# Two grouped convolution stages on 16 image pairs: float32 expansions on 17-row blocks, and one tap of nine multiplied on GpSimd

## The reference

```python
r  = relu(((x @ Wr + br) - mean) * rsqrt(var + eps) * gamma + beta)   # 64 -> 16 channels per pixel
w  = (r @ Ws + bs).reshape(B, H, W, 16, 1, 9)                          # nine weights per pixel and group of 4 channels
xi = x @ Wi + bi                                                       # 64 -> 64 channels
patches = nine shifts of zero-padded xi, reshaped (.., 16, 4, 9)       # channel-major: index = shift * 64 + channel
out = sum(w * patches, axis=-1)
```

## Time and profile before

| | us |
|---|---|
| median of 3 runs (lowest to highest) | 686.87 (686.27 to 687.97) |
| the profiled execution, its own time | 687.15 |
| its span in the trace | 685.4 |
| first expansion of the last stage | 463.50 |
| PE busy over the span | 649.0 (95%) |
| DVE busy | 551.1 (80%) |
| ACT busy | 287.1 (42%) |
| POOL busy | 172.6 (25%) |

### The profile page before, as it was taken

How to read it: one execution, slowest core, us unless ns; L and a number is a source line. 1 busy time by engine, 2 the same in 40 slices (tenths; PEclk the granted TensorE clock), 3 DMA queues, 4 the chain that set the end, 5 groups by cost and what they waited for, 6 DMA issues and landing times.

```text
span 685.4 us, 14823 instructions
## 1 busy us (share of the span) xinstructions
PE 649.0 (95%) x6176; PEld 265.6 (39%) x6176; DVE 551.1 (80%) x901; ACT 287.1 (42%) x370; POOL 172.6 (25%) x156
## 2 busy tenths in 40 slices
PE   6867999999999999999999989999999999999995
PEld 7533333333333333333333333333444444444542
DVE  5699866989988988995577787848888888888885
ACT  3754622323231422143102400043677777677661
POOL 2100420009102700450041110411344234234230
PEclk9999999999999999999999999999999999999998
DMA  9920000000000000000000000000011121121122
GB/s 327 214 56 1 2 1 1 1 1 2 2 1 1 2 1 1 1 2 1 1 13 4 1 1 2 1 1 1 20 44 33 42 52 33 34 60 33 32 62 63
DMA packets 54511, 19.67 MB, mean 29 GB/s; under 512 B 51154, under 2 KB 51892, under 8 KB 54452
## 3 DMA queue, kind: packets, MB, share of 16 engines
q1 hardware_dynamic: 54164, 18.57, 11.2%
q10 hardware_dynamic: 288, 0.21, 0.1%
HBM read 10.39 MB, written 8.39 MB: 27 GB/s over the span
## 4 chain that ended last, share of the span: by engine, by line
PE 72%; DVE 17%; ACT 1%; issue 1%; DVEq 0%; ACTq 0%
PE conv L670 36%; PE att L740 11%; PE conv L724 10%; PE att L460 4%; PE att L539 4%; DVE comb L1264 4%; DVE xpad L1183 3%; PE att L712 2%; PE att L551 2%; PE conv L636 2%; DVE x L1484 2%; DVE stats L1278 2%; PE att L518 1%; DVE x L1241 1%; DVE x L1240 1%
## 5 line engine op out<-in xcount | busy, mean ns | idle before, releaser
L670 PE MATMUL conv<-xpad,comb 64*64 64x512 f32 x2592 | 289.0, 593 | 4.8 <-DVE x L1248 2.9
L1484 DVE TENSOR_TENSOR x<-conv,x 128x512 f32<-128x512 f32 x288 | 179.0, 683 | 26.6 <-PE conv L724 25.3
L670 PEld LDWEIGHTS conv<-xpad,comb 64*64 64x64 f32 x2592 | 96.6, 133 | 173.7 <-issue 160.0
L1264 DVE SCALAR_TENSOR_TENSOR comb<-experts,wsel,comb 128x576 f32<-128x576 f32 (+1 forms) x138 | 112.8, 885 | 9.5 <-ACT comb L852 9.4
L724 PE MATMUL conv<-rstack,wse 98*128 98x512 f32 x288 | 96.3, 445 | 1.9 <-DVE xin L1273 0.9
L852 ACT ACTIVATE comb<-experts,wsel 128x576 f32<-128x576 f32 (+2 forms) x52 | 37.2, 768 | 112.7 <-PE conv L670 71.7
L740 PE MATMUL att<-x,cmp 64*32 64x512 f32 x1280 | 79.7, 596 | 0.0
L724 PEld LDWEIGHTS conv<-rstack,wse 98*128 98x128 f32 x288 | 49.5, 189 | 60.9 <-DVE x L1484 46.6
L1183 DVE SCALAR_TENSOR_TENSOR xpad<-att,x 128x1024 f32<-128x1024 f32 x46 | 53.9, 1214 | 19.8 <-PE att L518 19.6
L1621 POOL TENSOR_TENSOR x<-x,xin 128x1024 f32<-128x1024 f32 x15 | 35.9, 2396 | 115.2 <-ACT x L992 115.2
L862 ACT ACTIVATE x<-conv,bias 128x512 f32<-128x512 f32 x40 | 25.2, 681 | 83.5 <-PE conv L670 83.4
(11 more groups left out here) (186 smaller groups left out, 610.8 us busy)
## 6 DMA issues: line engine op xcount, KB each, us to landing
x<-in_x SPq DMA_DIRECT2D x32, 256.0 KB, 5.2
out<-comb SPq DMA_DIRECT2D x30, 256.0 KB, 3.2
experts<-in_We SPq DMA_DIRECT2D x1, 1152.0 KB
out<-comb SPq DMA_DIRECT2D x4, 128.0 KB, 2.2
wide<-in_c_wide SPq DMA_DIRECT2D x1, 192.0 KB, 5.6
x<-in_c_sum SPq DMA_DIRECT2D x1, 160.0 KB
small<-in_c_small ACTq DMA_DIRECT2D x1, 142.5 KB, 4.0
map_sel<-in_c_map SPq DMA_DIRECT2D x1, 128.0 KB
```

The lines of the kernel that those rows point to most:

```text
L670: last = nc.tensor.matmul(conv[own[to], h, HW * rows:HW * rows + HW], comb[own[rows], q % 2, n, tap(t)], xpad[own[rows], 2 * (q % 2) + n, ...
L1264: v.scalar_tensor_tensor(comb[:, q % 2, n, cols], experts[:, e, cols], wsel[:, p % 2, j + QP * n, e:e + 1], comb[:, q % 2, n, cols], ALU.m ...
L1484: v.tensor_tensor(img(prod[i])[:, rows, :], img(conv[:, unit, :])[:, rows, :], xip[s][:, kh + 16 * h:kh + 16 * h + 16, kw:kw + W], ALU.mul ...
```

## The change

- An expansion is now a plain float32 product on blocks of 17 rows (16 values of `r` and a one) by 64 columns (one image). The 128 partitions hold four copies in groups of 32: half 0 and half 1 for one `conv` unit, and again for the other. A half of a tap takes two matmuls, one for each image, so a tap takes four in place of two.
- `project` writes the four copies with eight matmuls of 64 rows by 32 columns in place of two of 128 by 96. The relu writes `rstack` at once, on 128 partitions; the row of ones comes out of it through its bias. ACT's rounded copy (L984) and POOL's `r_lo` are gone, and so is most of the making of the block weights.
- The centre tap moves from place 8 to place 2 (`SPARE`). Its expansion is copied out of PSUM by ACT in two halves (`empty_spare`), multiplied by POOL in two halves (`spare_product`) and summed last, as a round of its own. DVE makes the other eight products. Expansion 4 waits for ACT's copy. Sum rounds 1, 2 and 3 now take taps 3 and 4, 5 and 6, 7 and 8; before it was 2 and 3, 4 and 5, 6 and 7.

```diff
-ORDER = (0, 5, 1, 6, 2, 7, 3, 8, 4)
-ROUNDS = ((0, 1), (2, 3), (4, 5), (6, 7), (8,))
+ORDER = (0, 5, 4, 1, 6, 2, 7, 3, 8)
+SPARE = 2
+ROUNDS = ((0, 1), (3, 4), (5, 6), (7, 8), (SPARE,))
...
-            def project(k, s, m, weights, rows):
+            def project(k, s, m):
...
-                for h, cols in halves():
-                    last = nc.tensor.matmul(att[0:rows, 1, cols], weights, xn[s][:, cols], start=True, stop=True)
+                for copy in range(2):
+                    for n in range(2):
+                        for h, cols in halves():
+                            g = h + 2 * copy
+                            last = nc.tensor.matmul(att[RG * g:RG * g + RG, 1, HW * n:HW * n + HW], wr[own[n], :],
+                                                    xn[s][own[n], cols], start=True, stop=True)
...
             def expand(k, s, i):
...
-                        eng.wait_ge(prod_ready, 2 * (e - 2) + h + 1)
-                    nc.tensor.matmul(conv[:, unit, cols], wse[:, ORDER[i], :], rstk[s][0:RR, cols],
-                                     start=True, stop=True).then_inc(exp_full, 1)
+                        if i == SPARE + 2:
+                            eng.wait_ge(spare_emptied, 2 * k + h + 1)
+                        else:
+                            own_pair = i >= 2
+                            eng.wait_ge(prod_ready, 2 * products_to(k if own_pair else k - 1, i - 2 if own_pair else i - 2 + TAPS) + h + 1)
+                    first = RG * (h + 2 * unit)
+                    for n in range(2):
+                        last = nc.tensor.matmul(conv[own[n], unit, cols], wse[first:first + RR, ORDER[i], :],
+                                                rstk[s][first:first + RR, n, :], start=True, stop=True)
+                    last.then_inc(exp_full, 1)
...
-                eng.wait_ge(prod_ready, 2 * (k * TAPS + ROUNDS[r][-1] + 1))
+                if ROUNDS[r] == (SPARE,):
+                    eng.wait_ge(spare_ready, 2 * (k + 1))
+                else:
+                    eng.wait_ge(prod_ready, 2 * (products_to(k, ROUNDS[r][-1]) + 1))
...
+            def empty_spare(k, s):
+                unit = (s * TAPS + SPARE) % 2
+                if not (isinstance(k, int) and k == 0):
+                    eng.wait_ge(spare_ready, 2 * k)
+                for h, cols in halves():
+                    eng.wait_ge(exp_full, 2 * (k * TAPS + SPARE) + h + 1)
+                    nc.scalar.activation(spare[:, cols], conv[:, unit, cols], ACT.Copy).then_inc(spare_emptied, 1)
...
                 if not last:
                     normalise2(k + 1, 1 - s)
+                empty_spare(k, s)
                 if not first:
                     empty_sum(k - 1)
                 if not last:
-                    empty_r(k + 1, 1 - s, m)
+                    empty_r(1 - s, m)
                     empty_xi(1 - s, m + 1)
...
+            def spare_product(k, s):
+
+                if isinstance(k, int) and k == 0:
+                    eng.wait_ge(misc_free, 2)
+                else:
+                    eng.wait_ge(misc_free, 3 * k + 1)
+                    eng.wait_ge(sum_done, len(ROUNDS) * k)
+                kh, kw = divmod(ORDER[SPARE], 3)
+                for h in range(2):
+                    rows = slice(16 * h, 16 * h + 16)
+                    eng.wait_ge(spare_emptied, 2 * k + h + 1)
+                    v.tensor_tensor(img(prod[SPARE])[:, rows, :], img(spare)[:, rows, :],
+                                    xip[s][:, kh + 16 * h:kh + 16 * h + 16, kw:kw + W], ALU.mult).then_inc(spare_ready, 1)
...
             with eng.Fori(0, GP - 1) as i:
-                involve(2 * i + 1, 1)
-                involve(2 * i + 2, 0)
-            involve(NP - 1, 1, last=True)
+                spare_product(2 * i + 1, 1)
+                finish(2 * i)
+                spare_product(2 * i + 2, 0)
+                finish(2 * i + 1)
+            spare_product(NP - 1, 1)
+            finish(NP - 2)
```

More of the change, by code:

```diff
@@ L37 @@
 PARTS = 3
-AR = 96
-RR = 98
+RG = 32
+RR = 17
 T = S // 128
@@ L119, in chunk, with products_to @@
     return slice(c, GP, 2) if c < 2 else slice(CH * c, CH * c + CH)
-ORDER = (0, 5, 1, 6, 2, 7, 3, 8, 4)
-ROUNDS = ((0, 1), (2, 3), (4, 5), (6, 7), (8,))
-ROUND_OF = [r for r, made in enumerate(ROUNDS) for _ in made]
+ORDER = (0, 5, 4, 1, 6, 2, 7, 3, 8)
+SPARE = 2
+ROUNDS = ((0, 1), (3, 4), (5, 6), (7, 8), (SPARE,))
+ROUND_OF = [[i in made for made in ROUNDS].index(True) for i in range(TAPS)]
+def products_to(k, i):
+    return (TAPS - 1) * k + i - (i > SPARE)
 PARTS_OF_SUM = 4
@@ L201, in build @@
         st_sum = stage[:, 0:(TAPS + 1) * 32]
-        st_ws = stage[0:RR, 1152:1152 + TAPS * G16]
-        st_exp = stage[0:RR, 1296:1296 + TAPS * C]
-        st_bd = stage[0:RR, 1872:1872 + TAPS * 128].rearrange("p (t c) -> p t c", t=TAPS)
+        st_ws = stage[:, 1152:1152 + TAPS * G16]
         conv = ctx.enter_context(nc.psum_tensor("conv", [128, 2, S], F32))
@@ L294, in build @@
         pix = [pixels[:, n, :].rearrange("p (t c) -> p t c", t=T) for n in range(2)]
-        rstk = [rstack[:, n, :] for n in range(2)]
+        spare = row_sums[:, :, :, :, :].rearrange("p a b c d -> p (a b c d)")[:, 0:S]
+        rstk = [rstack[:, n, :, :] for n in range(2)]
         def sum_of(n, h):
@@ L349, in build @@
             (map_sel[:, :, :, :].rearrange("p j n c -> p (j n c)").bitcast(mybir.dt.uint16), A["c_map"]),
-            (masks[:, :], A["c_masks"]),
         ]
-        LATE_CONSTS = [(st_sum, A["c_sum"]), (st_ws[AR:RR, :], A["bs"].partition_broadcast(2))]
-        LATE_CONSTS += [(st_ws[CR * a:CR * a + CR, :], A["Ws"]) for a in range(2 * PARTS)]
+        LATE_CONSTS = [(st_sum, A["c_sum"])]
+        LATE_CONSTS += [(st_ws[RG * g:RG * g + CR, :], A["Ws"]) for g in range(4)]
+        LATE_CONSTS += [(st_ws[RG * g + CR:RG * g + RR, :], A["bs"].partition_broadcast(1)) for g in range(4)]
         BLOCKS = [(wi[64 * n:64 * n + 64, 64 * n:64 * n + 64], A["Wi"]) for n in range(2)]
-        BLOCKS += [(wr[64 * n:64 * n + 64, 32 * a + CR * n:32 * a + CR * n + CR], A["Wr"])
-                   for n in range(2) for a in range(PARTS)]
+        BLOCKS += [(wr[64 * n:64 * n + 64, 0:CR], A["Wr"]) for n in range(2)]
         CONSTS_IN = 16 * (len(CONSTS) + len(BLOCKS))
@@ L601, in beside @@
                         eng.wait_ge(att_free[1], sum(u == 1 for u, _ in ATT_USES))
-                        project(0, 0, 0, wr[:, :], AR)
+                        project(0, 0, 0)
                     elif at == (3, 1, 2):
@@ L755, in involve @@
                 if not last:
-                    project(k + 1, 1 - s, m, wr[:, :], AR)
+                    project(k + 1, 1 - s, m)
                 expand(k, s, 4)
@@ L894, in expanded_weights @@
                 late.then(nc.scalar.activation(
[L895 to L900, removed]
+                    wse[:, :, :].rearrange("p t c -> p (t c)").rearrange("p (g j t) -> p g j t", g=G16, j=C // G16),
+                    st_ws.rearrange("p (g t) -> p g t", g=G16).unsqueeze(2).to_broadcast([128, G16, C // G16, TAPS]), ACT.Copy))
                 late.then(nc.scalar.activation(sum_sel[:, :, :].rearrange("p a b -> p (a b)"), st_sum, ACT.Copy))
@@ L975, in empty_xi, with empty_r @@
                 done.then_inc(misc_free, 1)
-            def empty_r(k, s, m):
+            def empty_r(s, m):
                 eng.wait_ge(misc_full, m + 1)
[L979 to L984, removed]
+                nc.scalar.activation(rstk[s], att[:, 1, :].rearrange("p (n c) -> p n c", n=2), ACT.Relu, bias=rsc[:, 3:4],
+                                     scale=rsc[:, 1:2]).then_inc(misc_free, 1)
             def empty_sum(k):
@@ L1604, in _ @@
                 v.memset(xip[n], 0.0).then_inc(pads_zeroed, 1)
-                eng.wait_ge(pads_zeroed, 2 * n + 1)
-                v.memset(rstk[n][AR:RR, :].bitcast(F32), 1.0).then_inc(pads_zeroed, 1)
-                eng.wait_ge(pads_zeroed, 2 * n + 2)
+                eng.wait_ge(pads_zeroed, n + 1)
             inverse_root(4, slice(0, GP), GP)
[L1610 to L1616, removed]
             def finish(k):
@@ L1622, in finish @@
                 eng.wait_ge(fin_ready, k + 1)
[L1624 to L1632, removed]
+            def spare_product(k, s):
[10 more added lines that the diff above has]
+                                    xip[s][:, kh + 16 * h:kh + 16 * h + 16, kw:kw + W], ALU.mult).then_inc(spare_ready, 1)
+            spare_product(0, 0)
             inverse_root(5, slice(GP, NP), GP)
             with eng.Fori(0, GP - 1) as i:
-                involve(2 * i + 1, 1)
-                involve(2 * i + 2, 0)
-            involve(NP - 1, 1, last=True)
+                spare_product(2 * i + 1, 1)
[4 more added lines that the diff above has]
+            finish(NP - 2)
 def constants():
@@ L1683, in small_constants @@
         pick.reshape(128, -1), both(a["L0_conv_be"].T), all_rows(np.tril(np.ones((K, K)), -1)),
```

(2 more changed lines are left out.)

44 lines of the change are left out of this document (13 added, 31 removed).

## The result

| | before | after |
|---|---|---|
| median of 4 runs (lowest to highest), us | 686.84 (686.27 to 687.97) | 732.0 (729.23 to 734.54) |
| ratio, with 95% interval | | 1.065 (1.061 to 1.070) |
| the profiled execution, and its span | 687.15, 685.4 | 734.54, 733.0 |

The change makes the kernel 45 us slower. The forecast was 733, with a period of 16.08 us per pair in the last stage. The period in the trace is 15.66. The total came out closer than the period because three other terms, ahead of these periods and behind them, were off as well.

A forecast was written before the change was run, and what follows sets the result against it. PE was taken as the bound, DVE close behind. Fourteen periods of 16.08 in place of 13.02 us gave +42.3, pair 0 +1.0, the last pair +2.6: +45.9 on 687.15, so 733 us; range 718 to 766.

The forecast's parts named there:

- three other terms: Outside the 14 last-stage periods: weight setup before the stage 0, pair 0 +1.0 us, last pair +2.6 us.
- The rival of two goes: Expansion blocks: one row group at a time for two images, 0.86 us on each of four, 781 us; 4 in 100.
- latency: Last stage: float32 expansion results reach readers 0.66 us later at four exchanges (expansions 2, 6, 8, 1), 2.6 us per period.
- order: Last stage: the rest of 3.06 us per period, from ACT's copy ahead of the sum copies and the shifted sum round.
- The five expansion figures of the prediction: PE time of one pair's expansion blocks before the change: 1.04, 0.92, 1.13, 0.58 and 1.10 us, given as 4.9 together.
- PE's sum of work: PE's work per pair in the last stage, claimed to go from 13.0 to about 12.4 us.
- work decides: Last stage: waits hide behind each other, PE's work of 12.4 us becomes the period, 679 us in total; 5 in 100.
- the clock as a rival: Last stage: holes on PE drop the clock to half for a third of the time, +32 us, 765 us; 12 in 100.
- the removed setup: Making of block weights before the last stage: leaving it out gains 0, at best 1.4 us.

## Why the prediction was right, and where it was not

**The chain, step by step.** Starts after expansion 2 (595.64):

| step | forecast | trace |
|---|---|---|
| ACT's copy of tap 2 | 1.19 | 1.12 |
| sum copies | 2.41 | 2.09 |
| relu | 4.85 | 4.55 |
| `project_xi` | 6.11 | 5.81 |
| expansion 6 | 7.11 | 6.83 |
| product 6 | 8.30 | 7.95 |
| sum round 2 | 9.66 | 9.30 |
| expansion 8 | 10.66 | 10.32 |
| product 8 | 11.85 | 11.44 |
| sum round 3 | 14.21 | 13.79 |
| next expansion 2 | 16.08 | 15.66 |

Every link is there and in its order. The 0.42 too much is in two terms of the sum. A result reaches its reader 1.12 after the block's start, not 1.19 (three times 0.07 or so). Between the start of ACT's copy of tap 2 and the sum copies lie 0.97, not 1.22. I priced its two halves by the sum copies, 0.61 each, which start one after the other's end. The two halves of tap 2 take 0.60 each, but each overlaps the operation behind it by 0.1.

**One idle spell was mis-sized.** I had DVE idle for 2.6 ahead of product 6; it is 1.90. I started expansions 2 and 3 together at 0. The second half of expansion 3 waits for product 1, so `project` starts at 1.43 and not 1.0, expansions 4 and 5 at 2.45, and products 4 and 5 later. That moves idle from one place to another (1.04 ahead of product 4) and leaves the chain as it is.

**Blocks of 17 rows run like those of 64.** Expansion blocks of eight tiles take 1.02 to 1.04 with another shape behind (602.47 to 603.51), near the 1.00 of `project_xi`, and the eight start within 0.05 us (602.47 to 602.52). The rival of two goes is out. The Trainium skill, "TensorE: Matmul & The Clock Gate", section "The mechanism", lists that a weight load overlaps a running matmul only where the row group differs. The trace doesn't agree with that line: two images of one row group would have gone in turn, the second 0.86 later. The same section lets loads into a background weight buffer go ahead too; no run here tells whether that is what happens.

**What the period is made of.** The prediction put 2.6 of the 3.06 on latency and the rest, under 0.5, on order. Four kernels part the two:

| period, us | nine products on VectorE | tap 2 on GpSimd |
|---|---|---|
| expansions as before | 13.02 | 13.61 |
| float32 blocks, with their `project` | 14.80 | 15.66 |

The blocks cost 1.8 to 2.05 and the offload 0.6 to 0.86, so the prediction gave latency too much and order too little. It had said that 2.6 is "before any hiding", and part of it did hide. Swapping the copies gives 0.12 and moving expansion 8 gives 0.33. The single steps don't add up to one sum, since each removes a link and what stands beside it becomes the chain. How much of the blocks' price is latency and how much PE time no run parts.

**A slip without effect.** The five expansion figures of the prediction add to 4.77, not 4.9, and `project` stands there once as 1.8 and once as 1.6. With 4.77 and 1.8 PE's sum of work comes to 12.45, near the 12.4 used, and only the rival "work decides" hangs on it.

**The ends.** For pair 0 I took +1.0; it was +5.5. For the last pair I took +2.6; it was +7.1. The excess over the forecast is the clock. For the last pair that is shown below; for pair 0 it is likely for most of it. The prediction had the clock as a rival with 12 in 100 for the middle of the stage; in the middle it stayed at 1.00, at the ends it fell, and the forecast had no term for that. Two stretches of the changed kernel:

```profile
470.00:475.00 5.00, 5.00 (x48) 0.84 (x48) 2.80 (x6) 1.20 (x1) 0.00 (x0) 0.50 0.00 0
...
706.00:726.00 20.00, 16.87 (x138) 4.26 (x130) 9.34 (x15) 5.53 (x9) 4.71 (x3) 0.66 0.16 38
```

And the last pair of the run with GpSimd's product twice, whose order on PE is the same:

```profile
706.00:720.00 14.00, 10.41 (x130) 3.05 (x128) 8.97 (x15) 5.33 (x9) 7.06 (x5) 1.00 0.14 32
```

There expansion 2 of pair 15 stands at 704.61, the last sum is read at 718.43, 13.82 later (forecast 14.07), and the span ends at 727.7: 23.1 for the last pair, +2.5. So the term of the last pair was right, and 4.6 of its 7.1 is the clock. Pair 0 can't be parted as cleanly. It took 18.45 before with a mean granted clock of 0.91, 20.05 with 0.83 (expansion 8 first), 22.80 with 0.78 (GpSimd's product twice) and 23.91 with 0.71, so it grows as the clock falls, and no run of the changed order had 0.91. The clock also goes with the spread of 5 us in the changed kernel's four runs: 734.54, 733.78, 730.21 and 729.23 had a mean granted clock of 0.969, 0.972, 0.979 and 0.983. What makes it fall there wasn't taken apart.

**What I left out.** The last stage's first `project` runs inside the convolutions, where PE is the bound. It takes 1.02 to the next convolution row (450.14 to 451.16) in place of 1.89 (450.82 to 452.71). With 0.7 that the kernel had already gained by then (0.67 at 362 us), for which I have no cause, the stage begins 1.6 earlier. Part of that 0.7 can be spread between executions: the first expansion of the later profiles stands at 461.93 to 462.37 with the new `project`, and at 463.04 with the old one. I had looked at the removed setup for such a gain and not at `project`.

So the mechanism was right, its growth per period too large by 16% (3.06 against 2.64) and split wrongly between its two parts. That the total is right to 1 us (1.5 for the profiled execution) is luck: what was missed at the two ends (+4.5 each), in the periods (-5.7) and ahead of the stage (-1.6) nearly cancels.

## What to carry to other kernels

Where two engines hand each other half tiles through two buffers, an operation's latency counts, not its share of the array: blocks that leave TensorE's total work about as it was, but whose results come 0.6 us later, cost 1.8 to 2.05 us on a period of 13. Before work is moved off an engine, ask whether that engine is waited for; here relieving VectorE by one ninth cost 0.6 to 0.9 us per pair. The helper's copy needs a place in ScalarE's program, and neither place that was tried is cheap: ahead of the sum copies it holds back the sums, behind them it holds back expansion 4, and the two differ by 0.12. And a forecast is made by walking each engine's program from one fixed point through a period; the sum of work said 679.

## What the runs showed of the hardware

Float32 matmul blocks of 17 rows by 64 columns run eight at a time at the pace of 64 by 32 blocks (1.02 us for 512 columns, shape change included). The share of busy time doesn't tell whether the clock holds: with the sums copied first PE was, by the profile, busy 14.64 of 15.54 us (94%) and the clock fell in the next period, while the changed kernel kept 1.00 through the middle of the stage with PE busy 35.83 of 40 (90%). So a kernel with holes on TensorE can pay for them twice: that run took 748.9 in the median, though its full-clock period is shorter than the changed kernel's. GpSimd's product of two SBUF inputs took 1.20 for 512 columns, strided or not, and VectorE's products kept their pace beside it (1.29 for two halves at 596.88 with GpSimd busy, 1.29 at 607.08 with GpSimd idle).
